# Delta attention whose 128-token chunks are solved as two halves of 64, with the decay differences made a wave ahead

## What is computed

```
g_cum = cumsum(g);  decay = exp(tril(g_cum[:, None] - g_cum[None, :]))
L     = -(k * beta) @ k.T * decay          # strictly lower
attn  = inverse of (I - L)                 # by a triangular solve
v_intra = attn @ (v * beta);  k_cumdecay = attn @ (k * beta * exp(g_cum))
for each chunk in order:
    v_new = v_intra - k_cumdecay @ state
    out   = (q * exp(g)) @ state + (q @ k.T * decay) @ v_new
    state = state * exp(g_last) + (k * exp(g_last - g)).T @ v_new
out = rmsnorm(out * silu(z)) * norm_weight;  y = out @ W_out
```

## Time and profile before

| | |
|---|---|
| three timed runs | 2058.44, 2061.04 (median), 2062.00 us |
| the profiled execution | 2054.93 us, span 2053.1 us, 45861 instructions |
| mean granted clock of TensorE in it | 0.955 |
| busy over the span | PE 90%, DVE 63%, POOL 52%, ACT 48% |
| the loop over waves | from 940 us to the end |

### The profile page before, as it was taken

The page is one execution under the profiler, slowest core; times in us unless marked ns, Lnnn a source line. Parts: engine busy times, 40 slices in busy tenths (PEclk is TensorE's granted clock), DMA queues, the critical chain, the costliest instruction groups (busy, mean ns, idle before and its releaser), DMA issues.

```text
span 2053.1 us, 45861 instructions
## 1 busy us (share of the span) xinstructions
PE 1850.3 (90%) x16855; PEld 1191.3 (58%) x16855; DVE 1287.1 (63%) x2490; ACT 995.4 (48%) x2433; POOL 1072.0 (52%) x2252
## 2 busy tenths in 40 slices
PE   7799997867898885898999999999999999999987
PEld 5422664422244453445677777777777777677766
DVE  2544564685577422535777777777777777777753
ACT  2375232215321341434566656655665666566653
POOL 0521222323100302033888888887888878888873
PEclk7899999989999796899999999999999999999999
DMA  6044422200001333101222222222222222222221
GB/s 155 1 121 148 109 46 56 72 34 1 20 25 26 96 106 95 34 19 40 53 55 61 55 52 63 63 54 53 63 63 54 53 58 63 53 53 62 44 53 33
DMA packets 229260, 121.36 MB, mean 59 GB/s; under 512 B 141712, under 2 KB 208816, under 8 KB 228784
## 3 DMA queue, kind: packets, MB, share of 16 engines
q1 hardware_dynamic: 223424, 109.06, 21.3%
q0 software_dynamic: 5616, 9.38, 2.2%
HBM read 84.88 MB, written 36.68 MB: 59 GB/s over the span
## 4 chain that ended last, share of the span: by engine, by line
PE 22%; POOL 20%; issue 6%; SPq 3%; DVE 3%; DMA 3%; ACT 2%; POOLq 0%; DVEq 0%; ACTq 0%
POOL a_term L2594 8%; POOL a_z L2598 8%; PE ps L2046 5%; PE ps L2056 3%; PE ps L2245 3%; SPq L1979 2%; POOL a_rstd L2570 2%; POOL a_xnorm L2576 2%; DMA a_l<-a_v_dram 2%; PE ps L2276 2%; SPq L1987 1%; DVE a_v L2653 1%; PE ps L2212 1%; PE ps L2286 1%; PE ps L2221 1%
## 5 line engine op out<-in xcount | busy, mean ns | idle before, releaser
L2594 POOL TENSOR_TENSOR a_term<-a_z,a_l 32x14 f32<-32x14 f32 (+6 forms) x896 | 342.1, 382 | 70.3
L2598 POOL TENSOR_TENSOR a_z<-a_z,a_term 32x14 f32<-32x14 f32 (+6 forms) x896 | 341.7, 381 | 70.2
L2624 DVE SCALAR_TENSOR_TENSOR a_qkv<-a_raw,a_taps,a_qkv 128x1024 f32<-128x1024 f32 x192 | 247.0, 1286 | 6.1
L2046 PE MATMUL ps<-all_xn,a_w_qkv 128*128 128x512 f32 x512 | 246.9, 608 | 0.0
L388 POOL DMA_INDIRECT f_rows<-a_row,a_slots x32 | 35.7, 1116 | 192.1 <-DVE a_of_tile L377 146.7
L2245 PE MATMUL ps<-a_out_t,a_w_out 128*128 128x256 f32 x512 | 129.1, 395 | 1.9 <-ACT a_out_t L2468 1.7
L2046 PEld LDWEIGHTS ps<-all_xn,a_w_qkv 128*128 128x128 f32 x512 | 89.1, 193 | 69.3 <-issue 67.5
L2389 ACT ACTIVATE a_raw<-ps 128x512 f32<-128x512 f32 x128 | 76.3, 598 | 108.7 <-PE ps L2046 108.0
L2056 PE MATMUL ps<-a_w_z,all_xn 128*128 128x256 f32 x512 | 122.6, 383 | 0.0
L849 POOL DMA_INDIRECT f_sums<-a_y,a_xs x23 | 36.0, 1566 | 136.5 <-ACT a_y L798 133.5
L2588 POOL COPY a_z<-a_l 32x256 f32<-32x256 f32 x64 | 27.4, 429 | 152.3 <-DMA a_l<-a_v_dram 152.0
(11 more groups left out here) (331 smaller groups left out, 4303.7 us busy)
## 6 DMA issues: line engine op xcount, KB each, us to landing
a_gc_rows<-a_g_dram SPq DMA_DIRECT2D x64, 256.0 KB, 4.7
a_v_dram<-a_v SPq DMA_DIRECT2D x64, 256.0 KB
a_w<-in_f_w SPq DMA_DIRECT2D x24, 512.0 KB, 4.5
a_w_qkv<-in_a_w SPq DMA_DIRECT2D x16, 512.0 KB, 3.8
a_t_dram<-a_z SPq DMA_DIRECT2D x512, 8.0 KB
a_xs<-f_rows SPq DMA_DIRECT2D x46, 130.0 KB, 2.2
a_w_z<-in_a_w SPq DMA_DIRECT2D x16, 256.0 KB, 2.8
a_w_out<-in_a_wo SPq DMA_DIRECT2D x16, 256.0 KB, 3.1
```

Source lines behind the costliest of these rows:

```text
L2046: mm = pe.matmul(ps[:, to, :], w_qkv[:, k, mt * P:(mt + 1) * P], xn[:, k, b * T:(b + 1) * T], start=k == 0, stop=k == KC - 1)
L2594: pool.tensor_tensor(term[:, 0:j, j + 1:], z[:, 0:j, j:j + 1].broadcast_to([HP, j, n]), rows[:, j:j + 1, j + 1:].broadcast_to([HP, j, n]), ...
L2598: pool.tensor_tensor(z[:, 0:j, j + 1:], z[:, 0:j, j + 1:], term[:, 0:j, j + 1:], ALU.add).then_inc(sub_step, 1)
L2624: dve.scalar_tensor_tensor(to, rows, tap, to, ALU.mult, ALU.add).then_inc(conv_ready if j == TAPS - 1 else conv_step, 1)
```

## The change

The 128-token inverse is no longer made. Of it only the two 64-token diagonal blocks exist (`inv` is half as wide), and `join_c`, `close_c`, their three copies and `copy_z_half` go, with the third piece of `close_a` and of `close_b` that fed them. A new matrix `far` holds the scores times decay between the first and the second half. The solve is now in three steps for each wave: `solve_first` (first half), `first_values` (times beta; on ACT, on DVE for c = 0), `reach` (`far` times the first half's values), `settle` on DVE (subtract from the second half's right side), `solve_second`, `second_values` on ACT. `answer` and `grow_state` wait for the second half's values and come later in PE's order.

`make_low` becomes one addition on DVE, a wave earlier (w+3), and the own gate enters as the bias of four exponentials on ACT, at the end of the iteration. `square` moves behind them; `reduce` and `add_out` move from the end of DVE's iteration to the start of the next; `gated` and `carry` move to the end. `turn_out` writes a bank of its own (BX). `parts_of` gives 3, 2, 3 and 4 parts to c = 2, 3, 0 and 1.

```diff
-        inv = s.buf("inv", [P, 2, PR, P])
+        inv, far = s.buf("inv", [P, 2, PR, P // 2]), s.buf("far", [P, 4, PR, P // 2])
...
-            return [(g, t) for t in {2: (0, 1, 2), 3: (3, 4, 5), 0: (6, 7), 1: (8, 9, 10, 11)}[c]]
+            return [(g, t) for t in {2: (0, 1, 2), 3: (3, 4), 0: (5, 6, 7), 1: (8, 9, 10, 11)}[c]]
...
+                def solve_first(w):
...
                     for r in range(PR):
+                        right = v_row[FIRST, w % 4, r, :] if w % CH == 0 else rest[FIRST, r, :]
+                        mm = pe.matmul(bank(BR)[FIRST, r, :], inv[FIRST, w % 2, r, :], right, start=True, stop=True)
+                    mm.then_inc(x1_psum, 1)
+                def reach(w):
+                    pe.wait_ge(vnew1_ready, w + 1)
+                    pe.wait_ge(far_ready, w + 1)
+                    for r in range(PR):
+                        mm = pe.matmul(bank(BR)[SECOND, r, :], far[FIRST, w % 4, r, :], v_new[FIRST, r, :],
+                                       start=True, stop=True)
+                    mm.then_inc(far_psum, 1)
+                def solve_second(w):
+                    pe.wait_ge(settled, w + 1)
+                    for r in range(PR):
+                        mm = pe.matmul(bank(BR)[SECOND, r, :], inv[SECOND, w % 2, r, :], rest[SECOND, r, :],
+                                       start=True, stop=True)
+                    mm.then_inc(x2_psum, 1)
...
                 def make_decay(w):
-                    act.activation(decay[:, :, :], low[:, :, :], ACT.Exp).then_inc(decay_ready, 1)
+                    for r in range(PR):
+                        last = act.activation(decay[:, r, :], low[:, r, :], ACT.Exp, bias=gate(K_GC, w, r))
+                    last.then_inc(decay_ready, 1)
...
-                    for r in range(PR):
-                        dve.scalar_tensor_tensor(low[:, r, :], gc_rows[:, w % 2, r, :], gate(K_GC, w, r), floor[:, :],
-                                                 ALU.subtract, ALU.min).then_inc(low_ready, 1)
+                    dve.tensor_tensor(low[:, :, :], gc_rows[:, w % 2, :, :],
+                                      floor[:, :].unsqueeze(1).broadcast_to([P, PR, P]), ALU.add).then_inc(low_ready, 1)
```

The order of each engine's iteration, written out from the loops of the two kernels (- before, + after):

```
# PE, behind turn_values(w + 2)
-solve(w-1) part0 join_a(w) grow_state(w-1) close_a(w) answer(w-1) join_b(w) part1 close_b(w)
-turn_out(w-2) part2 turn_keys(w+2) join_c(w) project_out(w-2) part3 close_c(w)
+solve_first(w-1) part0 join_a(w) reach(w-1) close_a(w) part1 solve_second(w-1) join_b(w)
+turn_out(w-2) turn_keys(w+2) part2 close_b(w) answer(w-1) grow_state(w-1) part3 project_out(w-2)
# ACT
-make_decay(w+2) grow(w+2) new_values(w-1) part0 copy_tb make_values silu0 copy_wb part1 copy_half
-copy_out(w-2) square(w-1) silu1 copy_wc silu2 part2 silu3 copy_whole part3 make_keys(w+2)
+make_values(w+2) first_values(w-1) part0 silu0 copy_tb silu1 part1 second_values(w-1) copy_wb
+copy_out(w-2) make_keys(w+2) silu2 part2 copy_inv silu3 part3 make_decay(w+3) grow(w+3) square(w-1)
# DVE
-make_low(w+2) make_right(w-1) make_v0(w+2) widen(w) make_at close_wa make_qg copy_za carry(w-1)
-gated(w-1) conv0 copy_z_half conv1..3 reduce(w-1) add_out(w-2)
+add_out(w-3) reduce(w-2) make_right(w-1) make_v0(w+2) make_far(w+2) first_values(w-1, c=0) widen(w)
+make_at make_qg close_wa settle(w-1) copy_za conv0..3 make_low(w+3) gated(w-1) carry(w-1)
```

More of the change, by code:

```diff
@@ L2152, in close_b @@
                         for k in (0, 2):
[L2153 to L2156, removed]
+                            mm = pe.matmul(halves(BZ)[Q4[k], r, Q4[1]], wb[Q4[k + 1], r, :], za[Q4[k + 1], r, :],
+                                           start=True, stop=True)
                     mm.then_inc(b_psum, 1)
-                def join_c(w):
-                    pe.wait_ge(th_ready, w + 1)
-                    for r in range(PR):
[L2163 to L2172, removed]
-                                       start=True, stop=True)
-                    mm.then_inc(c_psum, 1)
                 def recall(w):
-                    if w >= 2:
-                        pe.wait_ge(ot_ready, w - 1)
                     if w % CH == 0:
@@ L2353, in _ @@
                     if made(w - 1):
-                        solve(w - 1)
+                        solve_first(w - 1)
                     part(w, 0)
@@ L2358, in _ @@
                     if made(w - 1):
-                        grow_state(w - 1)
+                        reach(w - 1)
                     if made(w):
                         close_a(w)
+                    part(w, 1)
+                    if made(w - 1):
+                        solve_second(w - 1)
+                    if made(w):
+                        join_b(w)
+                    if made(w - 2):
+                        turn_out(w - 2)
+                    if made(w + 2):
+                        turn_keys(w + 2)
+                    part(w, 2)
+                    if made(w):
+                        close_b(w)
                     if made(w - 1):
                         answer(w - 1)
-                    if made(w):
-                        join_b(w)
-                    part(w, 1)
-                    if made(w):
-                        close_b(w)
-                    if made(w - 2):
-                        turn_out(w - 2)
-                    part(w, 2)
-                    if made(w + 2):
-                        turn_keys(w + 2)
-                    if made(w):
-                        join_c(w)
+                        grow_state(w - 1)
+                    part(w, 3)
                     if made(w - 2):
                         project_out(w - 2)
-                    part(w, 3)
-                    if made(w):
-                        close_c(w)
             @block.scalar
@@ L2814, in _ @@
                 dve.wait_ge(gated_ready, F_TILES)
[L2815 to L2816 removed]
+                dve.memset(ps[:, BZ, :], 0.0).then_inc(cleared, 1)
                 f_add(1)
[L2818 removed]
+                for w in range(W + 3):
                     late = w % CH == 2
[L2820 to L2821 removed]
+                    if made(w - 3):
+                        add_out(w - 3)
+                    if made(w - 2):
+                        reduce(w - 2)
                     if made(w - 1):
@@ L2825, in _ @@
                         make_v0(w + 2)
+                        make_far(w + 2)
+                    if made(w - 1) and (w - 1) % CH == 0:
+                        first_values(w - 1)
                     if made(w):
```

206 lines of the change are left out of this document (108 added, 98 removed).

## The result

The changed kernel takes 2131.35 us (median of 4 runs, 2126.56 to 2134.80) against 2061.52 for the kernel before; the ratio is 1.0355, 95% interval 1.0327 to 1.0382. The forecast was 2083 with a range up to 2110: the direction is right, the size is not, 70 us slower instead of 22.

A forecast was written before the change was run, and what follows sets the result against it. The prediction took PE as the bound, busy for 90% of the span, with POOL's chain second. +1.15 us per head made +16 us over 14 heads; with +5.5 for the tail, 2061 + 22 = 2083 us, range 2050 to 2110.

The forecast's parts named there:

- PE's own work: PE's matmul groups in each head: added groups less removed ones and saved edges, +1.0 us per head.
- The new groups' price: `solve_first`, `reach` and `solve_second` on PE: 0.93 us each, between bounds of 0.89 and 1.04, 2.79 us per wave.
- The rival of the draining: Every meeting of 32x32 and 64x64 groups on PE drains: 2.4 us more per head, 2118 us; chance 12%.
- The waits that come: New PE waits per head: `project_out` 1.15, `solve_first` behind ACT's table load 1.2, `close_b` 0.4; +2.75 us.
- The tail: The last waves, without background work: 0.4 us for some four waves and 3.9 for the last, +5.5 us.
- The waits that go: PE's old waits in `turn_values`, `turn_keys` and `close_wa`, with others at the same places, counted as gone: -2.3 us per head.
- the chain over POOL: From DVE's `v0` through POOL to `xnorm`, 24.0 us: a head cannot fall far below 70 us.
- The rival of more speed: Cheaper 64x64 groups, hidden table load, overlapping waits: -1.5 us per head; 2045 to 2056 us, chance 22%.
- The recurrence as bound: `recall` to `carry`, 13.5 us, becomes the chain if PE's order delays links: 2100 to 2130 us, chance 6%.

The follow-up runs named there:

- e4: The changed kernel with the eight instructions of `reach` issued twice, same output; 2185.48 us, ratio 1.0607 to the kernel before.
- e2: The changed kernel with `reduce` moved on DVE behind `make_right`, `make_v0` and `make_far`; 2097.86 us, ratio 1.0175 to the kernel before.
- x2: The kernel before with only `ask`'s wait for bank BO moved behind its return for c = 0, `answer` waiting instead; 2060.35 us, ratio 1.0005.
- e3: The changed kernel with the output projection written to bank BX instead of BO, so it no longer waits for `gated`; 2172.79 us, ratio 1.0547.
- e23: The changed kernel with the changes of both e2 and e3; 2134.69 us, ratio 1.0370 to the kernel before.
- e8: e23 with POOL doing `root` and `normed` inside its substitution, ahead of step 10; 2126.43 us, ratio 1.0296 to the kernel before.
- x5: The kernel before with only `root` and `normed` moved into the middle of POOL's substitution; 2049.61 us, ratio 0.9942.
- x4: The kernel before with the moves of both x5 and x2; 2049.02 us, ratio 0.9950.
- x1: The kernel before with only `make_low` as one addition and four exponentials with bias, both a wave ahead; 2082.60 us, ratio 1.0114.
- e5: The changed kernel with two 512-column projections nobody reads in each of PE's last iterations; 2137.15 us, ratio 1.0380 to the kernel before.

## Why the prediction was wrong

Per head I forecast +1.15 us: +1.0 of PE's own work and +0.15 of waits. Measured are +3.9: about +2.5 of work, +0.9 of waits (both from the distances between starts of groups) and +0.5 of clock.

- **The new groups' price** was the first term that failed. I took 0.93 us for eight instructions on 64x64 pieces and said that two of three pay one edge at most; measured are 1.02 for each, 0.87 of columns and 0.15 for standing alone (e4). I also took off 0.11 us for `join_a`, which stayed. That is 12 x 0.09 + 4 x 0.11 = 1.5 us per head: PE's own work grew by 2.5, not by 1.0. The rival of the draining had this mechanism at 2.4 us more per head; the fact is 1.5, and it explains 21 us. But `solve_first` costs 1.02 between two full groups as well, where no 32x32 piece is near.
- **The waits that come** were right in place and too small. By distances, `solve_first` loses 1.55 us where I had 1.2, `project_out` 1.0, 0.4 and 0.15 where I had 0.95 and twice 0.1, `close_b` 0.35 for 0.4, and `xnorm` still 0.5 where I had left 0.25. That is 1.0 us per head more, of which the old waits, gone entirely, give back 0.2.
- **What a wait does to the clock** was missing. Of 14 heads 5, the first among them, run partly at half clock behind the wait for `a_rest`, 0.5 us per head in the mean. With the two points above this makes 1.5 + 0.8 + 0.5 = 2.8, against the 2.7 us per head that I was short. I had priced the wait at 1.2 us per head or 17 us in all, and removing it gave 33 (e2).
- **The tail** is the second large failure, 21 to 27 us for 5.5. I counted 0.4 us for each of four waves and 3.9 for the last, all at full clock. The granted clock there is 0.74. The same `solve_second` that takes 1.02 us takes 1.9 in five of the seven last waves. Filling shows that the clock can be had back; that most of the loss is its price is the estimate above. Why it falls just there is open. I can say only what stands ahead of it: groups on a quarter of the array and short waits, with no projections between. The kernel before has no projections there either, and 0.92 to 0.96.
- **The waits that go** went, but x2 shows that the way of counting was wrong. Taking `all_x`'s wait out of the kernel before gives nothing; other waits took its place. In e3, e23 and e8 a removed wait came back elsewhere, longer and with the clock. I had the chain over POOL in the text, used it to bound a gain, and did not use it to refuse credit for waits.
- **The rival of more speed** fell, and its counter-argument (the chain over POOL) is borne out in part: x5 and x4, which shorten that chain, are the only versions faster than the kernel before. Its other conditions failed too: the groups cost 1.02 us, not 0.89 or less, and the table load's delay was not hidden.
- **The recurrence as bound** did not come inside the heads.

What the parts give by themselves: the gates ahead +1.1% (x1); all together +3.5%; of that 1.6% are the place of `reduce`. Of e2's remaining 1.8%, 37 us between the medians, the two profiles (45 us apart) show 25 in the heads and 20 in the tail, of which some 6 are the short tail of the kernel before. In a head e2 has 2.5 us more of PE's work and 0.6 less of waits.

## What to carry to other kernels

A new matmul form is priced per group, not by its columns: count each change of piece size on TensorE, and run the form once in its place before rebuilding a loop around it. Where several engines' loops are interlocked, the length of a wait says little of what its removal gives: nothing (x2, another stands behind it), a loss (e3, 41 us, PE comes early to a longer wait and the granted clock falls with it), or more than its own length (e2, where the clock no longer fell behind it). Try it alone before crediting it. An operation that waits for an engine's table load must not stand ahead of the next link of a recurrence, even if it is 0.2 us long.

## What the hardware showed that was not expected

- Behind idle stretches of TensorE of 1.47 to 1.50 us the clock fell to half in 4 of 13 cases (the changed kernel), behind such of 1.6 to 2.3 us in 11 of 14 (x1). At 3.15 us (e3) it fell before the stretch ended.
- In the stretch without projections PE was busy for 108 of 129 us and yet at 0.74 of the clock; with 27 us of full-array matmuls more (e5) it was at 0.97 and the stretch was 3 us shorter.
- A group of eight 64x64 instructions of 128 columns costs 1.02 us alone and 0.87 behind its like (e4); a 128x128 one cost 0.89.
